# The scaled z and its two rounded parts made by GpSimd for both batches at once

## The reference

```
s = style @ mw.T + mb                         # one number per batch and input channel
weight = SCALE * w * s[:, None, :, None]
demod = rsqrt(sum(weight * weight, axis=(2, 3)) + EPS)
weight = weight * demod[:, :, None, None]     # so every batch has weights of its own
out = conv(x, weight) + b                     # same, upsample (+ blur), same, (blur +) downsample
...
x = x + ffn_i(cond_i(x, cond_512, ...))       # i = 0..3
```

## Time and profile before

| | |
|---|---|
| median of 3 runs | 2226.29 us (2222.68 to 2231.35) |
| profiled execution, its own time | 2228.09 us |
| its span, first to last instruction | 2226.2 us |
| TensorE busy | 2027.8 us (91%) |
| VectorE, ScalarE, GpSimd busy | 1194.4 (54%), 880.2 (40%), 425.6 us (19%) |
| mean granted TensorE clock | 0.968 of full speed |
| phases: first to last time of the pairs | layer 0: 60 to 300 us, layer 1: 398 to 820, layer 2: 1043 to 1507, layer 3: 1509 to 1787 |

### The profile page before, as it was taken

How to read it: one execution, slowest core, us unless ns; L and a number is a source line. 1 busy time by engine, 2 the same in 40 slices (tenths; PEclk the granted TensorE clock), 3 DMA queues, 4 the chain that set the end, 5 groups by cost and what they waited for, 6 DMA issues and landing times. The chain is left out here.

```text
span 2226.2 us, 29935 instructions
## 1 busy us (share of the span) xinstructions
PE 2027.8 (91%) x9750; PEld 1661.8 (75%) x9750; DVE 1194.4 (54%) x2001; ACT 880.2 (40%) x1352; POOL 425.6 (19%) x479
## 2 busy tenths in 40 slices
PE   2699967699999998998899999997999999979998
PEld 2577742588888877886788888876888778858886
DVE  4888879754455534233744544436555444454443
ACT  2377742444344322001433333323666544423441
POOL 4233311211111100111211111111000023342334
PEclk9899989899999999999899999998999999989999
DMA  6544525421122122224321111112111011132113
GB/s 154 170 136 137 144 90 207 158 76 57 57 76 66 57 95 85 94 94 124 110 69 62 57 57 57 57 48 81 38 34 32 19 52 47 45 129 82 49 43 155
DMA packets 100398, 189.11 MB, mean 85 GB/s; under 512 B 21377, under 2 KB 51073, under 8 KB 99585
## 3 DMA queue, kind: packets, MB, share of 16 engines
q1 hardware_dynamic: 99072, 186.55, 26.6%
q10 hardware_dynamic: 1280, 1.97, 0.4%
HBM read 126.02 MB, written 54.07 MB: 81 GB/s over the span
## 5 line engine op out<-in xcount | busy, mean ns | idle before, releaser
L938 PE MATMUL ps<-l_u_hi,l_g_hi 128*128 128x512 f32 x512 | 209.1, 408 | 22.7 <-DVE hmax L1291 21.6
L1100 ACT ACTIVATE l_hs<-ps,l_EY,dem3e 128x512 f32<-128x512 f32 x128 | 99.1, 777 | 306.5 <-PE ps L938 296.2
L938 PE MATMUL ps<-l_u_lo,l_g_hi 128*128 128x512 f32 x512 | 205.0, 400 | 0.0
L938 PE MATMUL ps<-l_u_hi,l_g_lo 128*128 128x512 f32 x512 | 204.7, 400 | 0.0
L119 POOL TENSOR_TENSOR l_hs<-l_EY,ones 128x4 f32<-128x4 f32 x128 | 34.6, 271 | 777.3 <-ACT l_hs L1100 777.3
L991 PE MATMUL ps<-l_w_hi,l_h_hi 128*128 128x512 f32 x512 | 166.3, 406 | 0.0
L2238 POOL TENSOR_TENSOR f_a_lo<-f_prod,f_a_hi 128x512 fp32r<-128x512 f32 (+1 forms) x88 | 113.5, 1290 | 269.3 <-ACT f_a_hi L2141 269.3
L991 PE MATMUL ps<-l_w_lo,l_h_hi 128*128 128x512 f32 x512 | 162.6, 399 | 0.0
L991 PE MATMUL ps<-l_w_hi,l_h_lo 128*128 128x512 f32 x512 | 162.3, 398 | 0.0
L2194 DVE SCALAR_TENSOR_TENSOR f_prod<-ps,b,f_gate 128x512 f32<-128x512 f32 (+1 forms) x88 | 66.0, 750 | 170.2 <-ACT f_gate L2134 170.2
L882 PE MATMUL ps<-l_x_hi,c_hi 128*128 128x512 f32 x256 | 109.7, 429 | 43.0 <-POOL l_u_lo L1582 43.0
(11 more groups left out here) (330 smaller groups left out, 4899.9 us busy)
## 6 DMA issues: line engine op xcount, KB each, us to landing
xin<-x SPq DMA_DIRECT2D x96, 256.0 KB, 4.0
l_xr<-x SPq DMA_DIRECT2D x32, 512.0 KB, 4.6
x<-l_xr SPq DMA_DIRECT2D x32, 512.0 KB, 2.6
v<-in_ffn_v SPq DMA_DIRECT2D x84, 128.0 KB, 2.7
xnat<-in_x SPq DMA_DIRECT2D x16, 512.0 KB, 4.0
xin<-xpl SPq DMA_DIRECT2D x64, 128.0 KB, 2.4
x<-xb SPq DMA_DIRECT2D x16, 512.0 KB, 4.6
q_xr<-x SPq DMA_DIRECT2D x16, 512.0 KB, 3.9
```

The source lines that it names most:

```text
L938: mm = nc.tensor.matmul(ps[:, 3 + h, :], Gs[ws][:, h, at:at + P], Us[ms][:, h, 1 + q:1 + q + HALF], start=(k == 0), stop=(k == 11))
L1100: nc.scalar.activation(hs[:, h, :], ps[:, 3 + h, :], ACT.Identity, bias=EY[:, 1, 0, bass.ds(h * NP + p, 1)], scale=dem3e[:, bass.ds(h * NP ...
```

## The change

In all four layers ScalarE's and VectorE's `split_z` are taken out, and GpSimd gets one. It is three instructions over both batches of the pair (2 x 192 = 384 numbers in a partition): the product into a new f32 buffer z_f, the copy rounded to hi, and the difference rounded to lo; each waits for the one before it. The zl semaphore now counts once for a pair. split_z(0) stands behind the first border zeroes and ahead of the last three memsets, split_z(1) behind these and ahead of layer 0's planes(1), and split_z(p+2) is the first thing in GpSimd's iteration p, ahead of planes(p+2) and patch(p).

```diff
@@ TensorE, weights_a @@
-                pe.wait_ge(zl_ready, 2 * (g0 + p) + 2)
+                pe.wait_ge(zl_ready, g0 + p + 1)
@@ ScalarE: gone, with its calls split_z(0), (1), (2) and (p + 2) @@
-            def split_z(p):
-                wait_pos(act, a_done, g0 + p)
-                for h in range(2):
-                    nc.scalar.activation(Zs[0][:, h, :, :], Z[:, :, :], ACT.Copy,
-                                         scale=column(s_v, p, h)).then_inc(zh_ready, 1)
@@ VectorE: gone, with its calls @@
-            def split_z(p):
-                for h in range(2):
-                    dve.wait_ge(zh_ready, 2 * (g0 + p) + h + 1)
-                    v.scalar_tensor_tensor(Zs[1][:, h, :, :]..., Z..., column(s_v, p, h),
-                                           Zs[0][:, h, :, :]..., ALU.mult,
-                                           ALU.subtract).then_inc(zl_ready, 1)
@@ GpSimd @@
+            def split_z(p):
+                wait_pos(pool, a_done, g0 + p)
+                flat = [t[:, :, :, :].rearrange("p h k c -> p h (k c)") for t in Zs]
+                row = Z[:, :, :].rearrange("p k c -> p (k c)").unsqueeze(1).broadcast_to([P, 2, TAPS * C])
+                g.tensor_tensor(z_f[:, :, :], row, outer(s_v[:, bass.ds(2 * p, 2)], TAPS * C),
+                                ALU.mult).then_inc(zf_ready, 1)
+                pool.wait_ge(zf_ready, g0 + p + 1)
+                carry_over(g, flat[0], z_f[:, :, :], ones[:, :]).then_inc(zh_ready, 1)
+                pool.wait_ge(zh_ready, g0 + p + 1)
+                g.tensor_tensor(flat[1], z_f[:, :, :], flat[0].bitcast(F32), ALU.subtract).then_inc(zl_ready, 1)
+
+            split_z(0)
             step(g.memset(pe_f[:, :, :], 0.0))
             step(g.memset(ve_f[:, :, :], 0.0))
             g.memset(EY[:, :, :, :], 0.0).then_inc(zeros_ready, 1)
+            split_z(1)
             if layer == 0:
 ...
             def iteration(p, first, ahead):
+                if ahead > 1:
+                    split_z(p + 2)
                 if layer == 0 and ahead > 1 and not first:
                     planes(p + 2)
                 patch(p)
```

More of the change, by code:

```diff
@@ L539, in conv_phase @@
         Zs = sb2("z", [P, 2, TAPS, C])
+        z_f = sb("z_f", [P, 2, TAPS * C])
         As = [sb("a_hi", [P, 2, 6 * C], F32R), sb("a_lo", [P, 2, 4 * C], F32R)]
@@ L655, in conv_phase @@
         xh_ready, xl_ready, zh_ready, zl_ready = sem("xh_ready"), sem("xl_ready"), sem("zh_ready"), sem("zl_ready")
+        zf_ready = sem("zf_ready")
         a_done, ah_ready, al_ready = sem("a_done"), sem("ah_ready"), sem("al_ready")
@@ L1148, in _ @@
             split_x(0)
-            split_z(0)
             read_u(0, 0)
@@ L1152, in _ @@
             read_a(0)
-            split_z(1)
             split_x(1)
@@ L1169, in first_pair @@
                 some_chunks(1)
-                split_z(2)
                 read_u(1, 0)
@@ L1200, in iteration @@
                     next_weights()
-                if ahead > 1:
-                    split_z(p + 2)
                 if layer == 0:
@@ L1252, in split_x @@
                                            ALU.subtract).then_inc(xl_ready, 1)
-            def split_z(p):
-                for h in range(2):
-                    dve.wait_ge(zh_ready, 2 * (g0 + p) + h + 1)
-                    v.scalar_tensor_tensor(Zs[1][:, h, :, :].rearrange("p k c -> p (k c)"),
-                                           Z[:, :, :].rearrange("p k c -> p (k c)"), column(s_v, p, h),
-                                           Zs[0][:, h, :, :].rearrange("p k c -> p (k c)").bitcast(F32), ALU.mult,
-                                           ALU.subtract).then_inc(zl_ready, 1)
             def read_a(p):
```

## The result

The changed kernel takes 2273.57 us (median of 4 runs, 2271.62 to 2275.73), the kernel before 2227.89 in the same series (4 runs, 2222.68 to 2231.35): ratio 1.0207, 95% interval 1.0184 to 1.0231. The change costs 45.7 us; 43 were forecast. The names in the rows stand for the steps of the text: l_g_f is written by sum_g, l_g_lo by split_g, l_x_lo by split_x, and l_qv, l_qm and wq by quantise. The *pitch* is the mean time from one start of biased to the next, *Z* the three new instructions, and a *turn* is time in which an instruction of GpSimd or VectorE stands blocked beside one of the other.

What follows compares the result with a forecast made beforehand. TensorE was taken as the bound (2027.8 of 2226.2 us), with a closed GpSimd and SyncE loop in layer 0. 27.7 (loop) + 7 (start) + 7 + 1.5 (first pairs) = 43 on 2226.3 gave 2270 us, range 2246 to 2290.

Steps and rivals of the forecast that it cites:

- Layer 0's loop: Layer 0's closed loop of planes, spread, store, landing and biased, lengthened by Z to 16.0 us a pair: +27.7 us.
- Start of layer 0: In layer 0, planes(1) stands behind split_z(1) and comes 6.9 us late, delaying TensorE's edges_p: +7 us.
- First pairs: First pair of each layer: split_z(2) delays patch(0), +3.5 us each in layers 1 and 2, +1.5 in layer 3.
- Steady pairs of layers 1 to 3: Later pairs of layers 1 to 3: Z falls beneath TensorE's matmuls and costs 0.
- hmax's wait: TensorE's wait for VectorE's hmax ahead of main_half in layer 0, 21.6 us in 15 waits: to be gone.
- The transposes' wait: TensorE's transposes waiting for GpSimd in layer 0: a new wait of 3 to 4 us a pair.
- VectorE's relief: Rival: in layer 0 VectorE's removed work shortens the path to hmax, -9 us there, 2218 us at best; chance 0.06.
- Only the edges: Rival: layer 0's loop shortens by other means, only starts and first pairs cost: +16, 2242 us; chance 0.08.
- Clock and turns: Rival: clock drops and full turns of VectorE make layer 0's pairs 17.2 us: +62, 2288 us; chance 0.13.

Runs made afterwards that it cites:

- e3: The changed kernel with layer 0's split_z(p+2) moved from ahead of planes to between the two halves of patch(p): 2246.90 us, ratio 1.0089.
- e6: The kernel before with three memsets of a dead buffer on GpSimd ahead of planes(p+2) in layer 0: 2246.97 us, ratio 1.0087.
- e8: The changed kernel with z's first product made twice in layer 0: 2285.84 us, ratio 1.0267.
- e2: The kernel before with the change in layers 1 to 3 alone: 2232.93 us, ratio 1.0015.
- e1: The kernel before with the change in layer 0 alone: 2267.66 us, ratio 1.0182.
- e5: The changed kernel with layer 0's split_z(p+2) between the patches, split_z(1) behind biased(1), and split_z(2) ahead of the wait for ey_ready: 2236.39 us, ratio 1.0048.
- e11: The kernel before with only SyncE's store_biased(p+1) put ahead of spread(p+2): 2243.81 us, ratio 1.0067.
- e12: The kernel before with the store ahead of spread and layer 0's biased(p+2) waiting for VectorE's g_lo of pair p+1: 2215.44 us, ratio 0.9953.
- e10: The changed kernel with store ahead of spread, layer 0's split_z(p+3) behind patch(p), split_z(1) behind biased(1), split_z(2) before the ey_ready wait: 2248.42 us, ratio 1.0091.

## Why the prediction was right

**Layer 0's loop** was the right mechanism (e3 takes z out of it, e6 and e8 put other work into it, and the pair follows each time) and its size was low: 27.7 us against 41.7 - 5.4 (start) = 36.3. The mis-sized term is the turns. Forecast: 8.1 from planes to the next biased, biased 2.41, 0.15, planes 1.89, Z 3.1, turns 0.4. Measured means: 8.05 + 2.80 + 2.39 + (1.16 + 0.93 + 1.17) + gaps of 0.14 = 16.64. Undisturbed (0.83 + 0.83 + 1.00 and 2.41, 1.89, by rows of this kernel where nothing stands beside them) it would be 15.2. So the part without turns was 0.4 us shorter than the forecast 15.6, 0.3 of it in Z, and the turns are 1.5 us, not 0.4. I had taken the value nearest to what planes lost before (0.29), with a bound of 1.6; with five GpSimd instructions back to back VectorE's second split_x and quantise instructions land between them wherever they are. Over the 11 spreads from spread(4) to spread(15), 132.92 to 315.35, that is (16.58 - 16.0) x 11 = 6.4 us, most of the miss of 8.6. Most of the rest lies behind spread(15), where the forecast took the tail of the layer as that of before. The transposes of pair 13 came at 316.52 and the start of layer 1 followed 123.74 us later instead of 121.44:

```profile
316.52 1.97 PE L949 MATMUL ps<-ident,l_hs 128*128 128x128 f32 x8 [3.12 <-POOL l_hs L119]
```

Over the 6 us from spread(15) the granted clock was 0.53, nearly all at 1.2 GHz.

**Start of layer 0**: +7 forecast, +5.4 found, by the same chain:

```profile
68.34 0.83 POOL L1571 TENSOR_TENSOR l_z_f<-Z,s_v 128x384 f32<-128x384 f32 x1 [1.18 <-PE ps L896]
...
71.13 2.21 POOL L119 TENSOR_TENSOR xpl<-xnat,ones 128x1024 f32<-128x1024 f32 x1
```

planes(1) is 5.4 us late, since z_f began 0.8 earlier than I had it (68.34, and not the 69.17 at which ScalarE's read_a starts) and Z took 2.8 instead of 3.3.

**First pairs**: 8.5 forecast. The wait for patch at the first pair is 5.1 us in layers 1 and 2 and 2.3 in layer 3 (the longest ones of L949 above), but the net's wait for h_lo behind it shrank (2.8 to 0.5 in layer 1), so layer 1 moved by 1.9. Layer 2 moved by 4.7, the rest by -1.9; together 4.6 instead of 8.5, and e2 has 3.7. The single stages are no finer than some 3 us: in the trace of e1, whose layer 1 is that of before, that layer is 2.7 us shorter (436.52 -> 1078.15 for 398.61 -> 1042.95). I had not asked what stood behind the stall and was late anyway.

So 43 + 8.6 (loop) - 1.6 (start) - 3.9 (first pairs) = 46: the total was nearer than its parts. That the misses cancel is luck.

**Steady pairs of layers 1 to 3**: nothing, as forecast, and in layer 3 also in detail:

```profile
1678.37 0.83 POOL L1571 TENSOR_TENSOR l_z_f<-Z,s_v 128x384 f32<-128x384 f32 x1 [3.62 <-PE ps L896]
...
1678.89 1.39 DVE L1263 TENSOR_TENSOR l_g_lo<-l_g_f,l_g_hi 128x1024 fp32r<-128x1024 f32 x1
...
1679.27 1.69 POOL L119 TENSOR_TENSOR l_z_hi<-l_z_f,ones 128x384 fp32r<-128x384 f32 x1
```

g_lo waited for the rest of z_f (1.39 instead of 1.23) and then z_hi for all of g_lo.

**Wrong in the signs to look for**: hmax's wait did not vanish (14.4 us in 10). By the rows of VectorE above, quantise, blocked beside GpSimd, makes sum_g and with it hmax late in such pairs. The transposes' wait was forecast at 3 to 4 us a pair in layer 0 and was 24.3 in 11 waits from 130 to 320. VectorE was not 50 us less busy but 21.6 more, through blocked time; ScalarE 41.6 less.

**The rivals.** *VectorE's relief* did not come: e3 and e5, with z out of the loop and off VectorE, have hmax's wait of 21.8 and 24.0 us, as before, and in e3's pair at 185 us quantise is blocked for 1.6 us, more than the 0.74 that z_lo had cost. *Only the edges* fell with e1, where layer 0 costs 38.4 us and its start only 5.4, and with the pitch of 16.64. *Clock and turns*: the turns were nearer to that case, and the clock did fall (0.91 over the pairs), but with a loop of 16.6 it was hidden in the pairs; in the tail it was not. In e11, where nothing else sets the pair, such a fall costs 1.55 us when it comes.

What stays open: e5's last 10 us in layer 0 are placed (3.3 by spread(4), 2.0 in the pairs, 4.6 behind them, with g_lo beside biased in the last pair), but no run took them away. Whether e12's wait would help e5, or e10, was not tried.

## What to carry to other kernels

Before an operation is moved to the idlest engine, look for the closed loop (buffer freed, transfer, next use) that this engine is in: an engine busy for 40% of a stage can have 0.8 us of slack in 13.3, and work put into the loop is paid in full, plus the turns, while the same work two calls later raised the pair by 0.4 us instead of 3.3. Count for a row of GpSimd instructions beside a busy VectorE the whole blocked instructions, not the smallest loss that one row shows. And when a wait is taken away, ask what it had kept apart: here the early store cost 15 us without a wait on the right producer and gained 12 with it, which no moved operation did.

## What was not expected of the hardware

- One f32 instruction of VectorE with two inputs in SBUF that starts beside one of GpSimd can be blocked for most of its listed length, and is listed as busy all that time: g_lo 2.83 for 1.23, wq 2.67 for 0.69. The busy share of an engine is not its work.
- In e11 every pair of layer 0 has a wait of 2.0 us ahead of main_half. In three of ten the granted clock then fell to 0.50 for about 3 us (0.89 over the pair), and in the others it stayed at 1.00, as it did from 130 to 270 us in the kernel before and in e12, where the waits were 1.1 and 0.4.
